# One 256x256 operator per chunk and batch in place of queries, head states and an output product, in a chunked ridge-attention block with a binarized FFN

## The reference

```python
def attn(x):                       # x = layernorm(input)
    xn = layernorm(x) * ln_g + ln_b
    q, k, v = xn @ Wq, xn @ Wk, xn @ Wv    # 256 -> 16 heads x 64, chunks of 128 rows
    # for each batch and head, S starts at zero, then for each of its 8 chunks:
    G = k.T @ k + 1e-4 * I
    W = solve(G, k.T @ v)
    U = I[:, :8]
    for _ in range(2):
        U, _ = qr(W @ U)
    S = 0.9 * S + U @ (U.T @ W)
    o = 0.125 * (q @ S)
    return x + o @ Wo
x = input + attn(layernorm(input))
h = gelu(layernorm(x) @ (alpha1 * sign(w1)).T + b1)     # exact, 256 -> 1024
out = x + h @ (alpha2 * sign(w2)).T + b2
```

## Time and profile before

| | before |
|---|---|
| runs, median (lowest to highest), us | 1051.5 (1044.22 to 1054.75) |
| profiled execution, us | 1048.18 |
| its span, us | 1046.3 |
| mean granted TensorE clock | 0.949 |
| TensorE busy | 945.3 us, 90% |
| VectorE busy | 656.5 us, 63% |
| ScalarE busy | 531.4 us, 51% |
| GpSimd busy | 196.3 us, 19% |
| instructions | 41030 |

### The profile page before, as it was taken

The page is one execution under the profiler, slowest core; times in us unless marked ns, Lnnn a source line. Parts: engine busy times, 40 slices in busy tenths (PEclk is TensorE's granted clock), DMA queues, the critical chain, the costliest instruction groups (busy, mean ns, idle before and its releaser), DMA issues.

```text
span 1046.3 us, 41030 instructions
## 1 busy us (share of the span) xinstructions
PE 945.3 (90%) x18210; PEld 716.2 (68%) x18210; DVE 656.5 (63%) x1439; ACT 531.4 (51%) x984; POOL 196.3 (19%) x246
## 2 busy tenths in 40 slices
PE   4999997999979988738997899989989999999997
PEld 2555554555645545637886778878878888888886
DVE  5774891699989996087786689887242263333333
ACT  2854443454545544413555545556656645555555
POOL 3332000101011000120120134211221132222223
PEclk9999998899989997859999999999999999999999
DMA  9553225635655665564354623434544211111100
GB/s 291 176 155 120 68 61 150 164 103 153 159 164 135 170 160 139 138 164 85 91 161 125 154 71 114 94 85 117 148 93 111 73 42 44 43 44 42 40 22 22
DMA packets 209632, 117.49 MB, mean 112 GB/s; under 512 B 144496, under 2 KB 196080, under 8 KB 208432
## 3 DMA queue, kind: packets, MB, share of 16 engines
q1 hardware_dynamic: 203984, 93.62, 34.7%
q0 software_dynamic: 5472, 21.24, 6.5%
HBM read 61.74 MB, written 53.08 MB: 110 GB/s over the span
## 4 chain that ended last, share of the span: by engine, by line
PE 71%; issue 11%; DVE 7%; DMA 5%; ACT 3%; SPq 2%; POOL 1%; POOLq 0%; DVEq 0%; ACTq 0%
PE psum L1134 15%; PE psum L1332 11%; PE psum L1144 10%; PE psum L1355 5%; PE psum L1365 5%; PE psum L1156 4%; PE psum L1321 3%; PE psum L1246 3%; PE psum L1307 2%; PE psum L1212 2%; PE psum L1199 2%; PE psum L1186 2%; DVE outer L997 2%; PE psum L1234 2%; PE psum L1294 2%
## 5 line engine op out<-in xcount | busy, mean ns | idle before, releaser
L1134 PE MATMUL psum<-wqkv,xhat 128*128 128x512 f32 x512 | 246.0, 625 | 6.2 <-ACT xhat L754 5.4
L997 DVE SCALAR_TENSOR_TENSOR outer<-sweep_mem,rd 128x992 f32<-128x992 f32 (+30 forms) x248 | 189.5, 764 | 8.7
L1003 DVE TENSOR_TENSOR sweep_mem<-sweep_mem,outer 128x992 f32<-128x992 f32 (+30 forms) x248 | 178.8, 721 | 8.5
L1134 PEld LDWEIGHTS psum<-wqkv,xhat 128*128 128x128 f32 x512 | 95.7, 197 | 110.5 <-issue 104.6
L762 ACT COPY kv<-psum 128x512 f32<-128x512 f32 x128 | 74.9, 586 | 128.5 <-PE psum L1134 128.3
L691 POOL TENSOR_TENSOR hsplit<-gc,hsplit 128x512 f16<-128x512 f32 x64 | 74.8, 1170 | 308.5 <-ACT hsplit L883 308.4
L1144 PE MATMUL psum<-xhat,wqkv 128*128 128x128 f32 x1024 | 128.2, 282 | 0.0
L1332 PE MATMUL psum<-wo,kv 128*128 128x256 f32 x512 | 125.8, 401 | 1.0 <-DVE state L1056 0.8
L1144 PEld LDWEIGHTS psum<-xhat,wqkv 128*128 128x128 f32 x1024 | 121.7, 197 | 2.6 <-issue 0.4
L1332 PEld LDWEIGHTS psum<-wo,kv 128*128 128x128 f32 x512 | 99.2, 199 | 17.2 <-DVE state L1056 1.3
L878 ACT ACTIVATE gc<-psum,b1c,alpha 128x128 f32<-128x128 f32 x256 | 96.5, 462 | 16.7 <-PE psum L1355 16.5
(11 more groups left out here) (117 smaller groups left out, 1302.3 us busy)
## 6 DMA issues: line engine op xcount, KB each, us to landing
gc_d<-gc SPq DMA_DIRECT2D x32, 512.0 KB, 3.2
schur_mem<-gc_d SPq DMA_DIRECT2D x32, 384.0 KB, 5.5
f_d<-fac SPq DMA_DIRECT2D x16, 544.0 KB, 3.7
fl<-f_d SPq DMA_DIRECT2D x32, 272.0 KB, 3.5
sv_d<-sv SPq DMA_DIRECT2D x16, 384.0 KB, 3.2
lead_d<-sweep_mem POOLq DMA_DIRECT2D x4, 1024.0 KB, 5.0
schur_mem<-lead_d SPq DMA_DIRECT2D x32, 128.0 KB, 5.0
r_d<-pt SPq DMA_DIRECT2D x16, 256.0 KB, 2.1
```

What stands on the lines that cost most here:

```text
L997: V.scalar_tensor_tensor(out=tile, in0=a[:, t, t + 1:HALF].unsqueeze(2).broadcast_to([P, m, HALF]), scalar=rd[:, t:t + 1], in1=a[:, t, t + ...
L1003: V.tensor_tensor(rest, rest, tile, ALU.subtract).then_inc(swept, 1)
L1134: ins = mm(dst[:], xnt[:, c, t], wqkv[:, n, t, BANK * half:BANK * (half + 1)], start=t == 0, stop=t == KT - 1)
```

## The change

**One operator per chunk.** Per head the output is 0.125 · xn Wq_h S_h Wo_h, summed over heads. The changed kernel no longer keeps S_h. The state of a batch is one 256x256 matrix M, the sum over heads of 0.125 Wq_h S_h Wo_h, which decays and grows by Σ 0.125 Wq_h Y (YᵀY)⁻¹ (YᵀW) Wo_h. Per pair of chunks, Wq_h Y (BQ, the query factors) and YᵀW Wo_h (BO, the output factors) are formed: 128 rows (16 heads of 8) of 256 columns each. Per turn NB multiplies the output factors by the inverses, which GpSimd has laid out block-diagonally (MB: four masked copies a batch into `mblock`), AU multiplies query factors and NB over 128 rows into the 256x256 increment, VectorE decays and adds it in one operation of 512 columns, and AT multiplies the normalized, transposed chunk by M. QA, QB, WRA, WRB, OT, WO and YT are gone. Wq is transposed once (QT, four steps from chunk 16 on). Y and Z have another layout: Y gives the 64x8 columns at once, Z gives WᵀY, again 64x8, and YᵀY, which has its own buffer in DRAM; MI becomes 16 small loads where it was four. SyncE's solve load is split in two (LS, LU); `pt` is double buffered, `x2b` has four buffers.

**Norms merged.** The two prelayernorms are computed from one set of moments: the second variance follows from the first, so VectorE makes moments once and GpSimd takes one power of var·(1+eps)+eps² ahead of xhat. What the residual needs (the first norm itself and its sum with the input) moves from VectorE to GpSimd.

**New order.** A list scheduler merges streams, in this order of precedence: the solve loads, two Schur chains, the projections, the solve's tail (Y, Z, BQ, BO), its lead (S, U, W, W), and the turns. The rule that picks among ripe sweeps is now a minimum of batch + 1.5 for a complement sweep. The order of the eight sweeps comes out the same.

The three places below are in the order of instructions on one engine; "x8" is a number of like instructions in a row.

The diff, cut to its core:

```diff
             ripe = [s for s in waiting if open_at.get(s, 1e9) <= now["pe"]]
             if ripe and len(staged) < 2:
-                s = max(ripe, key=lambda s: (s[0], -s[1]))
+                s = min(ripe, key=lambda s: s[1] + 1.5 * s[0])
...
+    def every(*steps, part=slice(None)):
+        return [(step, e) for e in range(NCH // 2)[part] for step in steps]
+
+    schur = [every("LC", "SP", "SX", "SV", part=slice(n, None, 2)) for n in range(2)]
+    loads = [every("LS"), every("LU")]
+    lead = [(step, 2 * e + n) if step == "W" else (step, e) for e in range(NCH // 2) for step, n in (("S", 0), ("U", 0), ("W", 0), ("W", 1))]
+    tail = every("Y", "Z", "BQ", "BO")
+
+    turn = []
+    for r in range(-4, turns + 3):
+        for step, n in (("LF", r + 4), ("LO1", r - 1), ("AT", r + 1), ("LR", r + 3), ("OUT", r - 2), ("X3", r + 1), ("NB", r + 2),
+                        ("HID", r), ("GE0", r), ("AU", r + 2), ("LO0", r), ("Y3", r + 1), ("GE1", r)):
+            if 0 <= n < turns:
+                turn.append((step, n))
...
+    streams = loads + schur + [main, tail, lead, turn]
+    while any(streams):
+        for stream in streams:
+            settle(stream)
+        heads = [stream for stream in streams if stream and stream[0][0] in BANKS]
...
                 elif step == "MI":
                     sp.wait_ge(minv_stored, 16 * (c + 1))
-                    src = minv_d[c].rearrange("(k q) i n -> q i k n", q=QUADS)
+                    if c >= 2:
+                        sp.wait_ge(m_blocked, QUADS * (c - 1))
+                    src = minv_d[c].rearrange("(u k q) i n -> q u i k n", u=QUADS, q=QUADS)
                     for q in range(QUADS):
-                        sp.dma_start(mi[HALF * q:HALF * q + RANK, c], src[q]).then_inc(mi_loaded[c], 16)
+                        for u in range(QUADS):
+                            at = HALF * q + RANK * u
+                            sp.dma_start(mi[at:at + RANK, c % 2], src[q, u]).then_inc(mi_loaded[c], 16)
...
+                n = g % 2
+                pool.wait_ge(spread_ready, g + 1)
+                if g:
+                    pool.wait_ge(hat_done, FIRST[g])
+                nc.gpsimd.tensor_tensor(rstd[:, 0:size], spread[:, n, 0:size], half_neg[:, 0:size], ALU.pow
                                         ).then_inc(rstd_ready, 1)
+                if g:
+                    pool.wait_ge(hat1_done, FIRST[g])
+                nc.gpsimd.tensor_scalar(first[:, 0, 0:size], mv[:, n, 0:size, 1], LN_EPS, None, ALU.add
+                                        ).then_inc(first_ready, 1)
+                pool.wait_ge(first_ready, 2 * g + 1)
+                nc.gpsimd.tensor_tensor(first[:, 1, 0:size], first[:, 0, 0:size], half_neg[:, 0:size], ALU.pow
+                                        ).then_inc(first_ready, 1)
...
+                for k in range(size):
+                    nc.gpsimd.tensor_scalar(lng[:, n, k], xg[:, n, k], mv[:, n, k, 0:1], first[:, 1, k:k + 1],
+                                            ALU.subtract, ALU.mult).then_inc(hat1_done, 1)
+                pool.wait_ge(hat1_done, FIRST[g] + size)
+                nc.gpsimd.tensor_tensor(lng[:, n, 0:size], lng[:, n, 0:size], xg[:, n, 0:size], ALU.add).then_inc(res_ready, 1)
...
+            def block_small(b):
+
...
+                pool.wait_ge(mi_loaded[b], 256)
+                if b >= 2:
+                    pool.wait_ge(*is_filled("NB", CPB * (b - 1) - 1))
+                for u in range(QUADS):
+                    nc.gpsimd.tensor_scalar(mblock[:, b % 2, :, RANK * u:RANK * (u + 1)], mi[:, b % 2], own[:, u:u + 1], None, ALU.mult
+                                            ).then_inc(m_blocked, 1)
...
-            def decay(r, h):
-
-                step = ("WRA", "WRB")[h]
-                dve.wait_ge(*is_filled(step, r))
-                src = place(step, r).rearrange("p (q n) -> p q n", q=2)[:, :, 0:2 * HD]
-                new, old = (state[:, n % 2, BANK // 2 * h:BANK // 2 * (h + 1)].rearrange("p (q n) -> p q n", q=2)
-                            for n in (r, r - 1))
+            def decay(r):
+                dve.wait_ge(*is_filled("AU", r))
+                src, new, old = place("AU", r), state[:, r % 2], state[:, (r - 1) % 2]
                 if r >= 2:
-                    dve.wait_ge(*is_filled("OT", r - 2))
+                    dve.wait_ge(*is_filled("AT", r - 2))
...
                     V.scalar_tensor_tensor(out=new, in0=old, scalar=DECAY, in1=src, op0=ALU.mult, op1=ALU.add
-                                           ).then_inc(drain(step, r), 1)
+                                           ).then_inc(drain("AU", r), 1)
...
+            def turn_query_weights(n):
...
+                dst = begin("QT", n)
+                for t in range(KT):
+                    nc.tensor.transpose(dst[:, P * t:P * (t + 1)], wq[:, t, 2 * P * n:2 * P * n + P], ident[:])
+                    for a in range(2):
+                        at, cols = DM + P * t, side(4 * n + 3 - a)
+                        ins = mm(dst[side(a), at:at + P], wq[:, t, cols], ident[:], start=True, stop=True)
+                ins.then_inc(fill("QT", n), 1)
...
+            def basis(e):
                 dst = begin("Y", e)
...
                 for c in range(2):
-                    for n in range(2):
...
+                    for q in range(QUADS):
+                        for n in range(2):
+                            at = RANK * (2 * (QUADS * c + q) + n)
+                            for a in range(2):
+                                ins = mm(dst[side(a), at:at + RANK], ww[side(a), c, 8 * n + 4 + q],
+                                         ww[side(a), c, 8 * n + q, 0:RANK], start=True, stop=True)
                 ins.then_inc(fill("Y", e), 1)

-            def basis(e):
-                dst = begin("YT", e)
+            def products(e):
+                dst = begin("Z", e)
                 pe.wait_ge(*is_drained("Y", e))
                 for c in range(2):
...
+                    for q in range(QUADS):
+                        for n in range(2):
+                            for a in range(2):
+                                at, own_at = BANK * n + RANK * (QUADS * c + q), RANK * (2 * n + a)
+                                ins = mm(dst[side(a ^ n), at:at + RANK], ww[side(a), c, 8 * n + q],
+                                         columns(y2, c, q, n)[side(a), own_at:own_at + RANK], start=True, stop=True)
                 for c in range(2):
                     for n in range(2):
...
+                            at, y = DM + HALF * c, columns(y2, c, q, n)
+                            ins = mm(dst[rows(q), at:at + HALF], y, y, start=n == 0, stop=n == 1)
                 ins.then_inc(fill("Z", e), 1)
+
+            def factors(step, e, thin, weights):
+
+                dst = begin(step, e)
+                for c in range(2):
+                    for n in range(2):
+                        for q in range(QUADS):
+                            ins = mm(dst[rows(q), DM * c:DM * (c + 1)], columns(thin, c, q, n), weights[:, 2 * q + n],
+                                     start=n == 0, stop=n == 1)
+                ins.then_inc(fill(step, e), 1)
...
             def apply_inverse(r):
                 c = TURNS[r]
                 b = c // CPB
-                dst = begin("NZ", r)
+                dst = begin("NB", r)
                 pe.wait_ge(fac_loaded[r % 3], 16 * (r // 3 + 1))
-                pe.wait_ge(mi_loaded[b], 64)
...
+                pe.wait_ge(m_blocked, QUADS * (b + 1))
+                for q in range(QUADS):
+                    ins = mm(dst[rows(q), 0:DM], mblock[rows(q), b % 2, c % CPB], fl[rows(q), r % 3, DM:], start=True, stop=True)
+                ins.then_inc(fill("NB", r), 1)
+
+            def operator(r):
+                dst = begin("AU", r)
+                pe.wait_ge(*is_drained("NB", r))
+                for t in range(KT):
+                    ins = mm(dst[:, DM * t:DM * (t + 1)], fl[:, r % 3, P * t:P * (t + 1)], nb[:, r % 2], start=True, stop=True)
+                ins.then_inc(fill("AU", r), 1)

             def attend(r):
...
+                dst = begin("AT", r)
+                pe.wait_ge(*is_drained("AU", r))
+                for t in range(KT):
+                    ins = mm(dst[:, 0:DM], xnt[:, TURNS[r], t], state[:, r % 2, DM * t:DM * (t + 1)],
+                             start=t == 0, stop=t == KT - 1)
+                ins.then_inc(fill("AT", r), 1)
```

610 lines of the change are left out of this document (260 added, 350 removed).

## The result

| | before | changed |
|---|---|---|
| runs beside each other, median (lowest to highest), us | 1047.86 (1043.5 to 1054.75) | 1010.99 (1007.37 to 1014.58) |
| profiled execution, us | 1048.18 | 1007.37 |
| its span, us | 1046.3 | 1005.6 |
| mean granted TensorE clock | 0.949 | 0.878 |
| TensorE busy | 945.3 | 841.9 |

The ratio is 0.9642, interval 0.9564 to 0.9721: faster, but outside the forecast range of 835 to 925 us. The profiled execution is 124.6 us longer than its forecast (span 1005.6 against 881), in two parts: the last sweep ends at 789.7 instead of 682.6 (107.1), and from there to the end it is 215.9 instead of 198.5 (17.4, and 0.1 of rounding).

What follows compares the result with a forecast made beforehand. VectorE's sweeps, no longer TensorE, were taken to set the time: the last sweep ends at 682.6, then 198.5 us to the end, a span of 881 and with 1.9 around it 883 us; range 835 to 925.

Steps and rivals of the forecast that it cites:

- the added work of twelve pairs is priced at nothing: Solve pairs before the last sweep's end: TensorE's added work hides behind VectorE's sweeps; without the room it would cost 49 us.
- A pair's price, 9.9: TensorE's solve of two chunks, S to BO: 9.9 us where it was 5.8, adding 65 us over 16 pairs.
- TensorE's cover, 240 us of work for 315: From last gram (368) to last sweep's end: TensorE has 240 us of work in 315, leaving 75 us of room.
- I see no wait for their load there.: VectorE's two small inversions before the last sweep's end: 7.2 us each, 14.4 together, with no wait for their load.
- The merged norm, "set at nothing": Start of second sweep, at 182.0: merged norm changes nothing; GpSimd under 7 us per group, up to 10 later if cover failed.
- Collisions, 12: VectorE's sweep work slowed beside GpSimd before the last sweep's end: 0.8 us a turn, 12 in all, between 0 and twice that.
- rival 4: Before the last sweep's end all GpSimd work holds VectorE up: 51 us in place of 12, giving 922; chance 0.08.
- The clock (rival 6): TensorE waiting on VectorE keeps its granted clock down: slower than before, past 1060 from mean clock 0.60 down; chance 0.03.
- TensorE's total: TensorE's work over the whole kernel: 233 us less in turns, 69 more in solves and turning Wq, net 164 less.
- cases 1 to 5: Whole time: forecast 865 to 900 (0.50), 839 (0.17), 905 (0.17), 922 (0.08), thin tiles one by one 1023 (0.03).
- the loop of power and low half: Late rounds: GpSimd's low half, then its power, then VectorE's split and Y3: 6.7 us, or 7.0 a round around two.
- The three rivals between 839 and 922: TensorE's 6.4 sets last rounds: 839 (0.17); VectorE keeps its 77%: 905 (0.17); GpSimd's work holds VectorE up: 922 (0.08).

Runs made afterwards that it cites:

- the best version: Solve's tail (Y, Z, BQ, BO) put ahead of Schur steps and projections in the order, against the kernel with measured planner costs (969.42): 956.94 us, ratio 0.9124.

## Why the prediction was wrong

Its step "the added work of twelve pairs is priced at nothing" failed, and with it the price of a pair. Point by point:

- **A pair's price, 9.9.** It was a sum of TensorE's products, and the forecast named the evictions between S, U, W, Y, Z and BO only for the first pair behind the last sweep. A pair took 17.8. In the one shown, 3.6 of the 7.8 too much are waits for ScalarE, 1.0 is Y, and 3.2 are the same products at a lower granted clock (0.78 over this pair). Doubling one eviction moved the pair by more than its own 2.1 and the end by 23.6, narrowing the products moved the pair by 0.8: that the pairs run as a chain with the evictions in it is shown. How waits and clock exchange isn't settled: narrower factors lowered the clock to 0.63, fillers raised it to 0.82, and neither moved the pair by 1 us.
- **TensorE's cover, 240 us of work for 315.** The room was counted as work against time, and a chain doesn't fill itself with later work: from the last Schur step to NB of turn 0 (458 to 541.0) there is nothing else for TensorE but pairs. Also the last gram came at 403.1, not 368. The 75 us of room were no room. With the longer eviction the eighth S came 18.4 us later, and the four pairs beside turns added nothing: cover does work, where there is some. When the order was written so that the last sweep ended at 679.4, 268.4 us were left behind it instead of 198.5: the pairs' time turns up on one side of that end or the other. 881 would have needed both, and no run had both: the best, at a span of 947.8, is still 67 over.
- **"I see no wait for their load there."** It was 32.2, and 16.7 at the first decay. This is the same failure seen from VectorE: the inversion needs four pairs, the turn the store, loads and masks behind it, whose loads stood 14 us in SyncE's queue (510.66 to 524.79). Planning the inversion later moved the wait and won 7, less than the intervals can tell.
- **The merged norm, "set at nothing".** 13.5 us on the second sweep. The risk was priced (up to 10 us if the cover fails) and rejected on "under 7 us per group" against 37 us of TensorE work. A group took 12.3, which would still have been covered by 37; what failed was again the order, since a memset that ScalarE needs stood behind the work for 16 chunks. Moving the branch to VectorE put the sweep at 181.0 and won 9 by the medians. The gap of 26.6 before the fourth sweep has a gram late behind Schur steps. With the old order it was 17.9, and 2.3 before the change; it stayed at 27.9 in the best version, and its own cause wasn't tried.
- **Collisions, 12.** VectorE's instructions took 22.7 us over their shortest between 541 and 790, beside 60.2 us of GpSimd's work, 1.5 a turn against 0.8. This is inside the range given, and rival 4 (all of GpSimd's time) was wrong: it would have been 60. The Trainium skill (SBUF — State Buffer, SBUF: two separate sides) has the later one wait for all of the other's instruction. The rows of L1105 agree: alone it takes 0.42; with 0.69 us of GpSimd's instruction left it took 0.97 (930.04), with 0.95 left 1.23 (922.68), and it ends 0.28 us behind GpSimd's each time. Over the stretch it came to 0.38 of GpSimd's time, because only the part that is left when VectorE arrives counts.
- **The clock (rival 6).** Its sign was right: 0.878 in the mean against 0.949, 0.73 around the pairs. The forecast's sum had no term for it. It is in 3.2 us of the pair shown; raising it to 0.82 there gave nothing.
- **TensorE's total.** 842 us busy where 945 less 164 gave 781. Sixteen times Y's 1.0 is 16 of the 61; the rest fits the lower clock but wasn't taken apart.
- **Slips in the sums.** The parts are 682.6 and 198.5, the line says 681 and 200; both give 881. The chances of cases 1 to 5 add up to 0.95, not 0.96.
- **Right:** sweeps of 54.7 each when fed; late rounds of 7.2 us by the loop of power and low half (7.0 forecast), and with that loop cut the next one, AT on the decay, 0.13 shorter; BQ, BO, NB (0.57), AU and AT (0.95, without the waits behind them) at full clock, so the packing of thin tiles. From the last sweep's end on it was 215.9 against 198.5, and 11 of the 17 are again in the pairs (the last BO ends 85 us behind the sweep, where 74 were forecast for the solve work with the turns between).

The three rivals between 839 and 922 all shared the failed step: each of them took the pairs as covered. A chance for "pairs run as a chain" was missing. The trace of before had a hint that wasn't taken: in the earlier trace rows U starts at 817.48 and Y at 827.58, ten microseconds for 1.2 of U and 2.0 of W, with the steps of a turn between them to fill the rest. Before turn 0 there are none.

## What to carry to other kernels

A step that is a chain of small products with an eviction between each costs its length, not its engine time, wherever nothing independent is ready beside it; so before work is called covered, list what the covering engine has ready in that stretch, in order. An order that is written by a cost table is only as good as the table's worst chain: comparing its own times with the trace's, step by step, showed where it drifted; with the table put right and one stream moved that was worth 45 us here (1001.55 to 956.94). Where an added operation is said to hide, price it from a row of the same operands: the per-partition operands made GpSimd's twice as dear as their width said.

## What was not expected of the hardware

Y has 64 products of 64x8 on two of the four 64x64 squares of the array and takes 1.97 us at full clock, 31 ns a product; Z has the same number of the same shape on all four and takes 1.04, 16 ns. W, with 64 columns a product on all four squares, takes 16 ns too (128 in 2.02 us). (Each of these is a recorded pass; an fp32 matmul has two.) The Trainium skill (TensorEngine Tiling (Array Packing), Key Properties) says that different tiles can load weights and multiply in parallel; these rows agree, and for 8 to 64 columns they fit a price that goes by the number of different squares and not by the columns. No run spread Y over four squares to test it.

GpSimd took 1.21 us for 256 columns with two per-partition operands and 2.35 for 1024 columns with two plain ones, 4.7 against 2.3 ns a column. Around the solve pairs TensorE was granted 0.73 of the full clock, 0.82 with fillers in its waits and 0.63 with narrower products; before the change it was 0.95 in the earlier trace rows, where turns and solves ran side by side.
